# TensorE's instruction stream in loops, expert rows transposed by the transfer, and the split of the hidden layer shared between VectorE and ScalarE

## The chip, the cores and the metric

The kernel runs on one core of one Trainium2 chip. The metric is the device time of one execution in microseconds (us), lower is better. The engines of the core are TensorE (PE; its weight loads are PEld), VectorE (DVE), ScalarE (ACT), GpSimd (POOL) and SyncE (SP); each has its own instruction queue ("q" behind its name in a row), and they meet only through semaphores.

## The reference

Two layers on x of 16 batches x 512 nodes x 128 features. The first is a graph attention (4 heads) with an adjacency mask, added to x. The second is a mixture of 8 experts, each token going to its best two:

```python
x = x + gat(layernorm(x), adj, W, a)            # softmax over neighbours, 4 heads of 32
z = layernorm(x)
gate_scores = einsum('bsd,ed->bse', z, Wg) + bg
topk_scores, topk_idx = top_k(gate_scores, 2)
combine = softmax(topk_scores) spread over the 8 experts
for e in range(8):
    h = relu(z @ W1[e].T + b1[e])               # 128 -> 512
    y = h @ W2[e].T + b2[e]                     # 512 -> 128
    out = out + combine[..., e] * y
return x + out
```

## The kernel before

One program with a hand-written stream for each engine. The first stage works in **slots**: slot s has the attention of batch s in its front part and the second normalisation, the routing and the placing of batches s-1 to s-4 behind it. `slots(eng, body, ahead, end)` unrolls a body for each slot, on TensorE 18 of them, two of which only drain. Inside TensorE's `body` the products of several batches are interleaved by hand: transposes, `products`, `gate`, `broadcast`, the row sums in pieces (`sums`) and `ranks`. Many have a wait whose value depends on the batch (`hold`, `ge`, `pe.wait_ge`); with the slots unrolled these values are constants. GpSimd writes the normalised rows of every token twice to DRAM (`xs`, L469), grouped by expert; a row is 128 high halves and 128 low halves in fp16 (together 128 fp32 words) and two fp32 words, the token's number and its first expert.

The second stage runs over `BLOCKS` = 71 **expert steps**. A block is 256 rows of one expert. Which rows and which expert a block has is in `tab`, which VectorE fills in two parts (`tab_ready` 1 for blocks 0 to 40, 2 from `FULL` = 41 on). The engines work at different blocks in one step n:

- SyncE (`load_rows`, L397 to 402) reads block n's row number from `tab` and loads its 256 rows (130 KB) into `xb`, one of four buffers. It first waits for the transposes (`bt_ready`) and the index (`bidx_ready`) of block n-4.
- TensorE (`layers`) transposes block n+3 (X, four transposes, L1529) into PSUM, then makes the up product of block n+2 (U, L1543): for each of four chunks of 128 hidden units three matmuls of 256 columns (high x high, high x low, low x high). Then it reads the expert number of block n+3 from `tab` (`expert`, L1514; numbers read before are handed on in `held`), and last makes the down product of block n (Y, L1560): 24 matmuls.
- ScalarE (`hidden`) copies the transposed rows to SBUF (`xt`, L662) and applies bias and ReLU to the up product, four activations into `h32` (L673).
- VectorE (`work`) computes the target rows (`bidx`, L1232), casts all of `h32` to fp16 (`hp[..., 0]`, L1222), subtracts to get the low half (L1224), and takes the down product out of PSUM into `ysb` (L1239), one of four buffers.
- GpSimd (`send`) scatters `ysb` to DRAM in two indirect transfers (L519); VectorE's output of block n+4 waits for them.

The order on TensorE in a step is thus transposes, up product, table read, down product, and the down product of a block comes two steps after its up product. The steps from -3 to 2 are laced with the last batches' routing; GpSimd scatters the last batches' rows between its first sends. After step 70 the results are loaded back, weighted, added to x and stored.

All steps and slots are unrolled in before. The one loop is SyncE's, which loads the adjacency of batches 2 to 15 in seven rounds of two (L388, the loads at L379). The class `Batch` holds a number that can be an integer or, in a loop, an expression of the round.

## Time and profile before

| | |
|---|---|
| median of 3 runs | 625.65 us (623.48 to 626.25) |
| the profiled execution | 624.53 us |
| its span, first to last instruction | 622.6 us |
| mean granted clock of TensorE | 0.928 of full speed |
| TensorE matmul busy | 477.3 us (77% of the span) |
| TensorE weight loads busy | 435.4 us (70%) |
| VectorE busy | 515.9 us (83%) |
| ScalarE busy | 447.7 us (72%) |
| GpSimd busy | 402.5 us (65%) |
| instructions | 22344 |

Busy time leaves out register, branch and semaphore instructions, and matmul ends are modelled. Behind a group or an instruction the profile writes the idle time of its engine before it and, with an arrow, who ended it; "issue" means that the engine waited for nothing that the profile shows. Shares over the whole span mix the slots, the expert steps and the final stage; the rows below are from parts of it.

### The profile page before, as it was taken

What the parts mean: (1) busy time and instruction counts of PE and PEld (TensorE: products, weight loads), DVE (VectorE), ACT (ScalarE), POOL (GpSimd) and SP (SyncE); (2) the same over time, 40 slices, a digit from 0 to 9 for tenths busy, and PEclk for the clock granted to TensorE, in tenths of its full rate; (3) what the DMA queues carried; (4) which work ended last, traced back from release to release, by engine and by line L of the source; (5) the groups of instructions that cost most, each with busy time, mean ns of one, the idle gap of its engine ahead of it and who ended that gap; (6) DMA issues with size and microseconds to landing.
All of it is one profiled execution on the core that took longest, in us unless ns stands there. A gap on an engine that the chain in (4) does not pass through costs nothing.

```text
span 622.6 us, 22344 instructions
## 1 busy us (share of the span) xinstructions
PE 477.3 (77%) x7450; PEld 435.4 (70%) x7509; DVE 515.9 (83%) x1619; ACT 447.7 (72%) x908; POOL 402.5 (65%) x342
## 2 busy tenths in 40 slices
PE   0687887977888787988867866799999999997000
PEld 0576787867888777988766755688888888887000
DVE  4689998999999999999988984678788888886297
ACT  1585778878888888998717745678888888884264
POOL 2241235887777777787776787878778887887300
PEclk9997999889989999999896998999999999999555
DMA  8922221222222233231113252233333323331499
GB/s 312 399 107 68 70 70 34 73 98 96 95 75 64 93 106 99 96 100 37 37 45 83 76 147 78 79 90 89 88 88 93 88 79 91 86 86 37 136 367 307
DMA packets 60781, 67.92 MB, mean 109 GB/s; under 512 B 7267, under 2 KB 46318, under 8 KB 60417
## 3 DMA queue, kind: packets, MB, share of 16 engines
q1 hardware_dynamic: 41936, 44.31, 22.9%
q0 software_dynamic: 8816, 17.46, 8.4%
q10 hardware_dynamic: 9920, 4.73, 2.6%
q8 instruction: 66, 1.08, 0.8%
q14 instruction: 43, 0.34, 0.2%
HBM read 44.16 MB, written 23.22 MB: 108 GB/s over the span
## 4 chain that ended last, share of the span: by engine, by line
issue 31%; DVE 29%; POOL 15%; PE 9%; DMA 8%; ACT 6%; POOLq 1%; SPq 1%; DVEq 0%; ACTq 0%
POOL expert_out L519 13%; PE bank L1369 4%; DVE edge L816 4%; DVE bs L719 3%; ACT xn L575 3%; DVE G L824 3%; DMA G<-in_L_ffn_W 2%; PE bank L1360 2%; DVE mv L722 2%; DMA adji<-expert_out 2%; POOL expert_rows L469 2%; DVE T L833 2%; DVE rowt L863 1%; DVE sc L759 1%; DMA G<-expert_out 1%
## 5 line engine op out<-in xcount | busy, mean ns | idle before, releaser
L519 POOL DMA_INDIRECT expert_out<-late,bidx x142 | 170.1, 1198 | 43.3 <-issue 42.7
L469 POOL DMA_INDIRECT expert_rows<-rowt,idx x128 | 156.6, 1223 | 40.6 <-issue 35.7
L570 ACT ACTIVATE G<-bank,s2c 128x512 uint8<-128x512 f32 x256 | 153.7, 703 | 0.0
L673 ACT ACTIVATE late<-bank,b1s,sc 128x256 f32<-128x256 f32 x284 | 137.3, 563 | 13.0 <-PE bank L1543 12.5
L1369 PE MATMUL bank<-V,G 128*128 128x66 bf16 x3072 | 131.1, 198 | 4.0 <-ACT G L570 0.5
L1369 PEld LDWEIGHTS bank<-V,G 128*128 128x128 fp8e4 x3072 | 121.0, 100 | 8.8 <-issue 1.6
L1560 PE MATMUL bank<-W2h,G 128*128 x1704 | 107.6, 220 | 20.2 <-DVE late L1239 18.7
L1560 PEld LDWEIGHTS bank<-W2h,G 128*128 128x128 f16 x1704 | 97.4, 98 | 36.2 <-issue 35.8
L1543 PE MATMUL bank<-late,W1h 128*128 128x256 f16 x852 | 107.1, 277 | 0.0
L1224 DVE TENSOR_TENSOR G<-late,G 128x1024 f16<-128x1024 f32 x71 | 87.0, 1226 | 2.4
L1543 PEld LDWEIGHTS bank<-late,W1h 128*128 x852 | 81.6, 99 | 9.1
L1360 PE MATMUL bank<-V,edge 128*128 128x132 bf16 x768 | 62.5, 234 | 26.5 <-DVE T L833 26.3
L1222 DVE CAST G<-late 128x1024 f16<-128x1024 f32 x71 | 49.7, 700 | 38.5 <-ACT late L673 38.5
L662 ACT ACTIVATE late<-bank 128x512 f16<-128x512 f16 x71 | 42.4, 597 | 42.4 <-PE bank L1529 38.6
L1360 PEld LDWEIGHTS bank<-V,edge 128*128 128x128 fp8e4 x768 | 53.0, 102 | 28.3 <-issue 28.1
L575 ACT ACTIVATE xn<-xr,nb,rs 128x128 f32<-128x128 f32 x128 | 51.7, 480 | 27.4 <-DVE nb L810 19.6
L459 POOL TENSOR_TENSOR V<-V 128x1056 f32<-128x1056 f32 x16 | 31.2, 1948 | 60.9 <-DVE V L941 50.6
L1239 DVE SCALAR_TENSOR_TENSOR late<-bank,sc,b2b 128x256 f32<-128x256 f32 x71 | 34.0, 479 | 9.7 <-DMA expert_out<-late,bidx 8.3
L824 DVE TENSOR_TENSOR G<-G,edge 128x2048 uint16<-128x2048 uint16 x32 | 38.8, 1212 | 0.6 <-ACT G L570 0.6
L1391 PE MATMUL bank<-Wr,xnT 128*128 128x128 f32 x128 | 31.4, 337 | 0.8 <-ACT xnT L594 0.7
L719 DVE BATCH_NORM_STATS2 bs<-xr 128x6 f32<-128x128 f32 x128 | 28.9, 277 | 3.7 <-DMA xr<-in_x 3.7
L1529 PE MATMUL bank<-identh,V 128*128 128x128 f16 x284 | 28.3, 223 | 0.0
(166 smaller groups left out, 688.9 us busy)
## 6 DMA issues: line engine op xcount, KB each, us to landing
adji<-in_adj SPq DMA_DIRECT2D x16, 1024.0 KB
V<-expert_rows SPq DMA_DIRECT2D x71, 130.0 KB
adji<-expert_out SPq DMA_DIRECT2D x8, 512.0 KB, 5.8
G<-expert_out SPq DMA_DIRECT2D x8, 512.0 KB, 8.4
expert_out<-late,bidx POOLq DMA_INDIRECT x142
G<-in_L_ffn_W SPq DMA_DIRECT2D x1, 2048.0 KB, 13.4
late<-in_L_ffn_W SPq DMA_DIRECT2D x1, 2048.0 KB, 10.1
expert_rows<-rowt,idx POOLq DMA_INDIRECT x128
```

The lines of the kernel that those rows point to most:

```text
L469: pool.indirect_dma_start(xs, bass.IndirectOffsetOnAxis(ap=idx[:, Z.q, k, j:j + 1], axis=0), rowt[:, Z.q, j, :], None).then_inc(scattered[ ...
L519: pool.indirect_dma_start(ybuf, bass.IndirectOffsetOnAxis(ap=bidx[:, B.o, t:t + 1], axis=0), ysb[:, B.q, t, :], None, bounds_check=2 * TOK ...
L570: act.activation(Gs[:, M.p, h // 2, mt, :, h % 2], zb[h][:, :], ACT.Sign, bias=s2c[:, M.p, mt, h:h + 1]).then_inc(S["z_used"], 1)
L575: act.activation(dst[:, j, :], src[:, j, :], ACT.Identity, bias=nb[:, bass.ds(first + j, 1)], scale=rs[:, bass.ds(first + j, 1)]).then_inc ...
L673: act.activation(h32[:, U.p, c, :], Up[U.p][c // 2][:, (c % 2) * BLK:(c % 2 + 1) * BLK], ACT.Relu, bias=b1s[:, bass.ds(ex * NC + c, 1)], s ...
L824: dve.tensor_tensor(w, w, edge[:, M.p].rearrange("p t n -> p (t n)"), ALU.bitwise_and) \
L1222: c.did(dve.tensor_copy(hp[:, U.q, 0], h32[:, U.p]))
L1224: c.did(dve.tensor_tensor(hp[:, U.q, 1], h32[:, U.p], hp[:, U.q, 0], ALU.subtract))
L1360: mm(o[:, :, HD + 1:VW], edge8[:, R.p, mt, nt * P:(nt + 1) * P], v[:, :, HD + 1:VW], start=(mt == 0 and q == 0), stop=False, skip_group_ch ...
L1369: last = mm(o[:, h, :], G8[:, R.p, h // 2, mt, nt * P:(nt + 1) * P, h % 2], v[:, h, :], start=False, stop=(part == H and mt == NT - 1 and ...
L1543: last = mm(o, w, xt[:, U.p, xq, :], start=(n == 0), stop=(n == 2))
L1560: last = mm(Yp(Y)[:, t, :], hp[:, Y.q, hq, c, t * P:(t + 1) * P], w[wq], start=(c == 0 and n == 0 and t == 0), stop=(c == NC - 1 and n == ...
```

## The change

Six edits, which belong together.

- TensorE's slots 6 to 15 become a loop of five rounds of two slots; slots 0 to 5 and the last two stay unrolled.
- TensorE's expert steps 17 to 64 become a loop of six rounds of eight steps (`UNROLL`); the others stay unrolled. In the first step of a round, and in step 65, the expert numbers of the blocks n, n+1 and n+2 are read again (`at.first`). TensorE waits for the second part of `tab` once before the loop.
- The rows of a block are loaded by a transposing transfer straight into `xt`, now four buffers, and the two words of each row by a second, plain transfer into `xb`. TensorE's four transposes and ScalarE's copy fall away; the up product waits for the transfers itself. SyncE waits for the up product of block n-4 in place of its transposes.
- VectorE makes the high halves of three of the four chunks, by a reduction over an axis of length 1 in place of the cast, as soon as three activations are done.
- ScalarE makes the high half of the fourth chunk with a fifth activation straight from PSUM; VectorE's subtraction waits for it.
- Counts of `hid_ready` and `ld_rows` change to match.

```diff
...
 SHARED = 16
+LOOP_STEP = SHARED + 1
+UNROLL = 8
+LOOPS = (BLOCKS - 3 - LOOP_STEP) // UNROLL
+LOOP_SLOT = 6
 SCALES = 17
...
 LN_STEPS, S_STEPS, MX_STEPS, ARG_STEPS, X_STEPS, ATT_STEPS, ROUTE_STEPS, PLACE_STEPS = 8, 5, 2, 6, 2, 4, 13, 9
...
         h32 = late[:, 0:2 * NC * BLK].rearrange("p (a c n) -> p a c n", a=2, c=NC)
...
             .rearrange("p (a q c n) -> p a q c n", a=4, q=2, c=NC)
-        xb = V[:, 0].rearrange("p q t h v -> p (q t h v)")[:, 0:4 * BT * ROW].rearrange("p (b t w) -> p b t w", b=4, t=BT)
+        xt = V[:, 0].rearrange("p q t h v -> p (q t h v)")[:, 0:4 * BLK].bitcast(FP16) \
+            .rearrange("p (a q n) -> p a q n", a=4, q=2)
+        xb = V[:, 0].rearrange("p q t h v -> p (q t h v)")[:, 4 * BLK:4 * BLK + 8 * BT].rearrange("p (b t w) -> p b t w", b=4, t=BT)
         ysb = late[:, 2 * NC * BLK:2 * NC * BLK + 4 * BT * D].rearrange("p (b t d) -> p b t d", b=4, t=BT)
-        xt = late[:, 2 * NC * BLK + 4 * BT * D:2 * NC * BLK + 4 * BT * D + 2 * BLK].bitcast(FP16) \
-            .rearrange("p (a q n) -> p a q n", a=2, q=2)
         bidx = sb("bidx", [P, 8, BT], I32)
...
             adji[:, :, :, :].rearrange("p a t n -> p (a t n)").bitcast(F32)
...
-            return XTb[1 if B.n < SHARED else B.p]
+            return XTb[1 if isinstance(B.n, int) and B.n < SHARED else B.p]
...
-            return Yb[1 if B.n < SHARED else B.p]
+            return Yb[1 if isinstance(B.n, int) and B.n < SHARED else B.p]
...
         names = """ld_const ld_small ld_w1 ld_w2 ld_x0 ld_x1 ld_x2 ld_adj0 ld_adj1
...
                 body(Batch(n))
...
-        def step(n):
-            return lambda k: Batch(n + k) if 0 <= n + k < BLOCKS else None
+        def step(n, first=False):
+            at = lambda k: Batch(n + k) if 0 <= n + k < BLOCKS else None
+            at.first = first
+            return at
+        def looped_step(u, i):
+            at = lambda k: Batch(LOOP_STEP + u + k, i, UNROLL)
+            at.first = u == 0
+            return at
+        def is_block(B, n):
+            return isinstance(B.n, int) and B.n == n
+        def early(B):
+            return isinstance(B.n, int) and B.n < SHARED
...
             eng.wait_ge(S["ends_ready"], 1)
...
                 sp.wait_ge(scattered[k], 16 * 2 * NT * EARLY // 4)
...
             def load_rows(B):
-                ge(sp, S["bt_ready"], B.n - 3)
+                ge(sp, S["up_ready"], (B.n - 3) * NC)
                 ge(sp, S["bidx_ready"], B.n - 3)
                 r = sp.value_load(tab[0:1, 0, bass.ds(B.n, 1)], min_val=0, max_val=E * CAP)
-                sp.dma_start(xb[:, B.q], xs[bass.ds(r, BLK), :].rearrange("(t p) w -> p t w", p=P)) \
+                sp.dma_start(xt[:, B.q], xs[bass.ds(r, BLK), 0:D].bitcast(FP16), transpose=True) \
+                  .then_inc(ld_rows[B.q], 16)
+                sp.dma_start(xb[:, B.q], xs[bass.ds(r, BLK), D:ROW].rearrange("(t p) w -> p t w", p=P)) \
                   .then_inc(ld_rows[B.q], 16)
...
                 if n == FULL:
...
                 X, U = at(3), at(2)
-                if X:
-                    act.wait_ge(S["bt_ready"], X.n + 1)
-                    ge(act, S["up_ready"], (X.n - 1) * NC)
-                    if X.n == 0:
-                        act.wait_ge(S["w_dve"], 2 * PIECES)
-                    act.activation(xt[:, X.p], XTp(X), ACT.Copy).then_inc(S["xt_ready"], 1)
                 if U:
...
                     if U.n == 0:
...
                         act.activation(h32[:, U.p, c, :], Up[U.p][c // 2][:, (c % 2) * BLK:(c % 2 + 1) * BLK],
...
                            .then_inc(S["hid_ready"], 1)
+                    ge(act, S["down_ready"], U.n - 3)
+                    act.activation(hp[:, U.q, 0, NC - 1], Up[U.p][1][:, BLK:2 * BLK], ACT.Relu,
+                                   bias=b1s[:, bass.ds(ex * NC + NC - 1, 1)], scale=sc[:, 10:11]) \
+                       .then_inc(S["hid_ready"], 1)
             b13, b14, b15 = Batch(NB - 3), Batch(NB - 2), Batch(NB - 1)
...
             copy_x2T(b14)
...
-                dve.wait_ge(S["hid_ready"], U.n * NC + NC)
+                dve.wait_ge(S["hid_ready"], U.n * (NC + 1) + NC - 1)
                 ge(dve, S["down_ready"], U.n - 3)
                 c = Chain(dve, S["split_steps"], 2, U.n)
-                c.did(dve.tensor_copy(hp[:, U.q, 0], h32[:, U.p]))
+                c.did(dve.tensor_reduce(hp[:, U.q, 0, 0:NC - 1], h32[:, U.p, 0:NC - 1].unsqueeze(3), AX.X, ALU.max))
+                dve.wait_ge(S["hid_ready"], U.n * (NC + 1) + NC + 1)
                 c.wait()
...
                 U, Y = at(2), at(0)
...
-                    dve.wait_ge(ld_rows[U.q], U.f * 16 + 16)
+                    dve.wait_ge(ld_rows[U.q], U.f * 32 + 32)
                     ge(dve, back[U.q], (U.f - 1) * 16 * BT)
-                    dve.scalar_tensor_tensor(bidx[:, U.o, :], xb[:, U.q, :, D + 1], tf[:, 5, bass.ds(U.n, 1)],
-                                             xb[:, U.q, :, D], ALU.not_equal, ALU.add).then_inc(S["bidx_ready"], 1)
+                    dve.scalar_tensor_tensor(bidx[:, U.o, :], xb[:, U.q, :, 1], tf[:, 5, bass.ds(U.n, 1)],
+                                             xb[:, U.q, :, 0], ALU.not_equal, ALU.add).then_inc(S["bidx_ready"], 1)
                     split(U)
...
                     ex = dve.value_load(tab[0:1, 1, bass.ds(Y.n, 1)], min_val=0, max_val=E - 1)
...
                     ge(pe, S["route_steps"], (m4.n - 1) * ROUTE_STEPS + 1)
...
                         pe.wait_ge(S["place_steps"], m5.n * PLACE_STEPS + 3)
-                    if m4.n == 0:
+                    if at.s == 4:
                         pe.wait_ge(S["scale_steps"], 3)
...
                 if at.s == 3:
...
                     sums(m1, 0, 3)
...
                     weight_rows()
-            slots(pe, body, 0, NB + 2)
+            def at_slot(n, i=None):
+                if i is None:
+                    at = lambda k: Batch(n + k) if 0 <= n + k < NB else None
+                    at.s = n
+                else:
+                    at = lambda k: Batch(n + k, i)
+                    at.s = None
+                return at
+            for n in range(LOOP_SLOT):
+                body(at_slot(n))
+            with pe.Fori(0, (NB - LOOP_SLOT) // 2) as i:
+                body(at_slot(LOOP_SLOT, i))
+                body(at_slot(LOOP_SLOT + 1, i))
+            for n in range(NB, NB + 2):
+                body(at_slot(n))
...
             def layers(at):
...
                 X, U, Y = at(3), at(2), at(0)
-                if X:
-                    pe.wait_ge(ld_rows[X.q], X.f * 16 + 16)
-                    ge(pe, S["xt_ready"], X.n if X.n < SHARED else X.n - 1)
-                    if X.n == 0:
-                        pe.wait_ge(S["v_steps"], NB * X_STEPS)
-                    if X.n == SHARED:
-                        pe.wait_ge(S["xn2T_ready"], NB)
-                    xv = xb[:, X.q, :, 0:D].bitcast(FP16).rearrange("p t (q d) -> p t q d", q=2)
-                    for q in range(2):
-                        for t in range(BT):
-                            last = pe.transpose(XTp(X)[:, q, t * P:(t + 1) * P], xv[:, t, q, :], identh[:, :])
-                    last.then_inc(S["bt_ready"], 1)
-                ey, ex = held[0], held[2]
+                ey, ex = held[0], expert(U) if at.first else held[2]
                 if U:
-                    if U.n == 0:
+                    if is_block(U, 0):
                         pe.wait_ge(S["w_dve"], 2 * PIECES)
...
                         pe.wait_ge(S["t_steps"], NB * NT)
-                    pe.wait_ge(S["xt_ready"], U.n + 1)
-                    ge(pe, S["hid_ready"], (U.n - 1) * NC)
+                    pe.wait_ge(ld_rows[U.q], U.f * 32 + 32)
+                    ge(pe, S["hid_ready"], (U.n - 1) * (NC + 1))
                     for c in range(NC):
...
                             w = W1h[:, wq, bass.ds(ex, 1), c * P:(c + 1) * P].rearrange("p e h -> p (e h)")
-                            last = mm(o, w, xt[:, U.p, xq, :], start=(n == 0), stop=(n == 2))
+                            last = mm(o, w, xt[:, U.q, xq, :], start=(n == 0), stop=(n == 2))
                         last.then_inc(S["up_ready"], 1)
-                if X and X.n == FULL:
-                    pe.wait_ge(S["tab_ready"], 2)
+                if at.first:
+                    ey = expert(Y)
+                    held[1:] = [expert(at(1)), ex]
                 held[:] = held[1:] + [expert(X) if X else None]
                 if Y:
-                    if Y.n == 0:
+                    if is_block(Y, 0):
                         pe.wait_ge(S["arg_steps"], NB * ARG_STEPS)
                         pe.wait_ge(S["rows_ready"], NB)
-                    if Y.n == SHARED:
+                    if is_block(Y, SHARED):
                         pe.wait_ge(S["place_steps"], NB * PLACE_STEPS)
                     pe.wait_ge(S["split_steps"], Y.n * 2 + 2)
-                    ge(pe, S["y_ready"], Y.n if Y.n < SHARED else Y.n - 1)
+                    ge(pe, S["y_ready"], Y.n if early(Y) else Y.n - 1)
                     for c in range(NC):
...
                         for n, (hq, wq) in enumerate(((0, 0), (1, 0), (0, 1))):
...
             layers(step(1))
...
             ranks_after(b15)
-            for n in range(3, BLOCKS):
+            for n in range(3, LOOP_STEP):
                 layers(step(n))
+            pe.wait_ge(S["tab_ready"], 2)
+            with pe.Fori(0, LOOPS) as i:
+                for u in range(UNROLL):
+                    layers(looped_step(u, i))
+            for n in range(LOOP_STEP + LOOPS * UNROLL, BLOCKS):
+                layers(step(n, n == LOOP_STEP + LOOPS * UNROLL))
...
 _INS = ["x", "adj", "L0_gnn_W", "L0_gnn_a", "L0_ffn_Wg", "L0_ffn_bg", "L0_ffn_W1", "L0_ffn_b1", "L0_ffn_W2", "L0_ffn_b2"]
```

## Rows read from the trace of the kernel before

**Rows 1.** Waits, 200 to 300 us: us in total, times, longest.

```profile
PE bank L1360 <- DVE T L833: 8.9, 6, 2.2
...
PE bank L1405 <- DVE mxp L899: 4.3, 5, 0.9
...
DVE g L959 <- PE bank L1398: 0.6, 1, 0.6
```

**Rows 2.** Windows: length, busy us (instructions) of PE, PEld, DVE, ACT, POOL; clock, DMA.

```profile
404.00:566.00 162.00, 160.14 (x2129) 141.92 (x2130) 129.99 (x213) 134.06 (x266) 129.40 (x108) 1.00 0.31 86
```

**Rows 3.** Timeline of TensorE's weight loads: start, us, what, idle before.

```profile
404.52 1.35 PEld L1560 LDWEIGHTS bank<-W2h,G 128*128 128x128 f16 x24 [1.34 <-issue]
...
486.39 1.35 PEld L1560 LDWEIGHTS bank<-W2h,G 128*128 128x128 f16 x24 [0.16 <-issue]
...
487.93 1.25 PEld L1543 LDWEIGHTS bank<-late,W1h 128*128 x12
489.51 0.18 PEld L1560 LDWEIGHTS bank<-W2h,G 128*128 128x128 f16 x3 [0.34 <-issue]
...
565.51 1.36 PEld L1560 LDWEIGHTS bank<-W2h,G 128*128 128x128 f16 x24 [0.30 <-issue]
...
568.08 2.77 PEld L1560 LDWEIGHTS bank<-W2h,G 128*128 128x128 f16 x48
```

**Rows 4.** TensorE's queue by line, 486.3 to 489.42 us: ns min/median/max, first and last start.

```profile
L1560 PEldq ALU_OP  x8: 32/32/32, 486.3 to 487.1; - x8
...
L1543 PEldq FUSED_REGOPS  x8: 46/46/46, 487.7 to 488.5; - x8
...
L1514 PEldq TENSOR_LOAD <-tab x1: 303/303/303, 488.7 to 488.7; - x1
```

**Rows 5.** Timeline of all engines, the end of the expert steps.

```profile
574.02 0.48 DVE L1239 SCALAR_TENSOR_TENSOR late<-bank,sc,b2b 128x256 f32<-128x256 f32 x1 [1.35 <-PE bank L1560]
...
581.92 0.98 POOL L519 DMA_INDIRECT expert_out<-late,bidx  x1 [0.30 <-issue]
```

**Rows 6.** Timeline, single instructions: reductions, transfers, cast and activations.

```profile
17.69 4.42 DVE L759 TENSOR_REDUCE sc<-G 128x1 f32<-128x4096 f32 x1 [1.27 <-DMA G<-in_L_ffn_W]
...
344.65 1.96 POOL L469 DMA_INDIRECT expert_rows<-rowt,idx  x1 [1.10 <-DVE rowt L1022]
...
364.09 0.99 POOL L519 DMA_INDIRECT expert_out<-late,bidx  x1 [0.31 <-issue]
...
364.57 0.41 DVE L1054 TENSOR_REDUCE tf<-cube 128x31 f32<-128x248 f32 x1
...
451.51 0.69 DVE L1222 CAST G<-late 128x1024 f16<-128x1024 f32 x1 [0.57 <-ACT late L673]
451.60 1.46 POOL L519 DMA_INDIRECT expert_out<-late,bidx  x1 [0.30 <-issue]
...
452.60 1.93 ACT L673 ACTIVATE late<-bank,b1s,sc 128x256 f32<-128x256 f32 x4 [0.16 <-PE bank L1543]
```

**Rows 7.** Waits, 342 to 404 us.

```profile
PE bank L1560 <- DVE late L1239: 16.3, 10, 3.5
DVE late L1239 <- DMA expert_out<-late,bidx: 8.3, 4, 3.6
```

**Rows 8.** SyncE's queue, the loop of adjacency loads (L388, L379).

```profile
L388 SPq FUSED_REGOPS  x7: 50/50/64, 24.4 to 236.2; - x7
...
L388 SPq COMPARE_BRANCH  x7: 44/45/50, 46.4 to 270.8; - x7
...
L379 SPq FUSED_REGOPS  x14: 46/46/57, 32.3 to 270.2; - x14
```

**Rows 9.** Waits of SyncE's queue over the whole span.

```profile
SPq L107 <- DVE bidx L1232: 142.2, 65, 6.4
```

**Rows 10.** DMA view: a queue (packets, MB, share); an issue (KB, us to landing).

```profile
q8 instruction: 66, 1.08, 0.8%
...
xr<-in_x SPq DMA_DIRECT2D x1, 256.0 KB, 2.9
```

## The prediction

> **What bounds the kernel now.** The program has stages with different limits, so I first cut its span into windows. The attention slots run to about 320 us, the expert steps from 342 to 575 us, and then come the last loads, sums and stores, which the change leaves alone. In the slots the waits tell the bound: VectorE waits once in 100 us, for 0.6 us, while TensorE waits 8.9 us for VectorE's sums and 4.3 us for its row maxima [rows 1]. At some 18 us a slot (seven rounds of two slots in SyncE's loop, 46 to 271 us [rows 8]) that is 2.4 us of slack a slot on TensorE.
>
> From 404 to 566 us TensorE is "busy" 160 of 162 us [rows 2], but its ends are modelled, so I read its weight loads instead. The loads of the down product begin at 404.52 and, 53 steps later, at 565.51 us: 3.04 us a step [rows 3]. In one step, the down product and the four transposes take 486.39 to 487.93, the up product 1.25 us, and then comes a gap of 0.34 us that no engine releases ("issue"); the step before had one of 0.16 [rows 3]. The last full step with neither a transpose nor a table read goes from 565.51 to 568.08 with no gap: 2.57 us [rows 3]. So neither the array nor another engine is the bound; TensorE's own sequencer is. The same step in its queue [rows 4]: eight register operations of the down product start from 486.3 to 487.1, a pitch of 0.12 us and 0.96 in all; waits and transposes fill the time from there to 487.7, where eight fused register operations of the up product follow at the same pitch, another 0.96; then the table read for a later step starts at 488.7, and its check and a wait last until just before the next down product's first load at 489.51 [rows 3]. Nothing stands still. From the two products I solve the prices. Down: 48 loads and matmuls and 8 x 0.032 us in 0.96, so an array instruction costs 0.0147 us. Up: 24 x 0.0147 and eight fused operations in 0.96, so one of these costs 0.076, its gap included. A table read costs 0.7 us.
>
> The other engines have room. VectorE is busy 130 of 162 us, 2.45 a step, and waits for ScalarE the rest; ScalarE 134 us [rows 2]. GpSimd's gaps are all "issue", never data, yet it stays two sends behind: after the last output (574.02 + 0.48) its last transfer starts at 581.92 [rows 5], so it ends at 582.9.
>
> **Transposes and copy go.** TensorE's sequencer loses what fills 487.26 to 487.7 [rows 4], less one wait that stays: about 0.30 us. ScalarE loses one copy a step and gains a fifth activation of 1.93 / 4 = 0.48 us [rows 6]: about even, and off the path. An unrolled step would cost 3.04 - 0.30 = 2.74 us.
>
> **The split.** The cast of 1024 elements (0.69 us [rows 6]) becomes a reduction of 768. Reductions take 4.42 us for 4096 elements and 0.41 for 248 [rows 6]: 1.04 ns an element and 0.15 fixed, so 0.95 us, 0.26 more. VectorE's step becomes 2.45 + 0.26 and some 0.1 for semaphores, 2.8 us: below TensorE's pace, free in the loop, but the floor of an unrolled step. What it buys is GpSimd's time. A send that begins under the cast (451.60, cast from 451.51) lasts 1.46 us; one with a reduction inside it (364.57, in the send of 364.09) lasts 0.99 [rows 6]. But the subtraction that follows the cast holds sends as well: the transfer of 344.65, begun just after a subtraction had started, takes 1.96 us [rows 6]. So GpSimd can stay stretched and two sends behind. At the end: a send right after the last output would finish at 574.5 + 0.3 + 2.3 = 577.1 instead of 582.9, so 0 to -5.8 us; I take -2, nearer to nothing since the subtraction stays. From 342 to 404 us TensorE waits 16.3 us for VectorE's output, 8.3 of it because VectorE waits for sends [rows 7]; against that gain stands 0.26 us more on VectorE in a dozen steps. +3 to -8 us; I take -3.
>
> **The expert loop.** 48 of the 71 steps (17 to 64) become six rounds of eight. Their wait values (rows landed, activations, split, outputs) and the table address now depend on the round: five quantities a step. The nearest row is SyncE's loop of adjacency loads: two waits and two addresses a round, for which seven rounds pay 14 + 7 fused operations, three for four quantities [rows 8]. That makes 3.75 x 0.076 = 0.28 us a step; bounds 0.1 (values shared within a round) and 0.38. At the head of each round three expert numbers that unrolled code carries over are read again: 3 x 0.7 = 2.1 us, 0.26 a step. The loop's own counter and branch are one operation each in eight steps, 0.01. The step becomes 3.04 - 0.30 + 0.28 + 0.26 + 0.01 = 3.29 us, over VectorE's floor of 2.8, and +0.25 x 48 = +12 us. Nothing covers it: the array already waits for this sequencer in each step. Queued behind are the up product, ScalarE's activations, the split, the outputs and the sends. Step 65 repeats the three reads (+2.1), and some six unrolled steps at full pace gain 0.25 each (-1.5). The wait for the table's second half moves from step 38 to step 17; VectorE sets that flag after its sixth step, so it costs nothing.
>
> **The slot loop.** Ten slots become five rounds of two. Some 40 waits a slot get register values: at 3/4 of 0.05 to 0.076 us, 1.5 to 2.3 us of sequencer, against 2.4 us of waiting [rows 1]. Most of it hides there, but VectorE has no idle time to absorb results that come late. Bounds 0 and +1 us a slot; I take +0.3, +3 us in all.
>
> **The transfers.** SyncE waits mostly for VectorE's index, 142 us over 65 loads [rows 9], so the queue has time, for a second transfer too. The rows are now used by the up product, one step after the transposes used them, so the load's lead grows by about 3 us, and the load waits for an up product three rows back, which is done when the index is. The trace has no transposing transfer; bounds: a plain load like today's, or one longer than a step. I take the first, zero. The Trainium skill ("Advanced Engine Details and Errata", X-Bar Transpose) says that transposing transfers on trn2 are as fast as ordinary ones; no row here shows it, and it would leave the sum as it is.
>
> **Sum.** +12 + 2.1 - 1.5 + 3 - 3 - 2 = +10.6, on the profiled run's 624.5 us (its span of 622.6 and 1.9 around it) 635; that run stands 1.1 below the median of 625.65, so 636.
>
> **Rivals.** (1) *Refetched code*: each jump back must bring the loop's first instructions again while TensorE stands still. Its code came in 66 blocks over the span, which took 0.8% of 16 engines' time, 1.2 us each; a 256 KB load lands in 2.9 us [rows 10]. So 1.2 to 3 us a jump, six in the steps, and five in the slots, where waiting hides half: 636 + 6 x 2.5 + 5 x 1.2 = 657. The Trainium skill ("Runtime: NRT & Kernel Launch", Instruction fetch mechanics) says that a taken branch to a target outside the fetched window stalls until its page is there; SyncE's loop is too short to show it, and here the bodies are some 850 and 1,300 instructions. (2) *Half price*: wait values are shared and the reads at the head overlap the array's backlog. Then the step is 3.02 us, and the gains of ramp and end stand against the slots: 624. (3) *The sequencer is no bound once the transposes are gone*: VectorE's floor of 2.8 us sets the step, 54 x -0.24 = -13, with -5 before 404 us and -3 at the end: 604. This is the case on the other side; it decides if a looped step's register work and reads stay under 0.06 us. Against it stands the gap in every step; for it, that the fifth activation and the shorter reduction relieve VectorE, which pays only where VectorE is the bound, and that GpSimd has no idle time of its own now. (4) *The transposing transfer takes longer than a step*, say 4 us: TensorE waits for rows in 66 steps, 690. It decides above 3 us.
>
> **Chances.** Forecast 0.42 (its own range 628 to 650), refetch 0.14, half price 0.15, VectorE's floor 0.22, slow transfer 0.07. Within 0.5%, about what a measurement of this kernel can tell from no change, is 622.5 to 628.8: most of the half-price case and an edge of the forecast, 0.16; slower 0.56; faster 0.28. The range reaches from just below the fast case to the refetch case, 602 to 660.
>
> **What would show it.** Right: the first loads of the down product stand 3.0 to 3.1 us apart inside a round with some 2 us extra at every eighth, "issue" still before them, more fused operations a step and four table reads at a round's head; no send stretched to 1.46 by a cast. Wrong: gaps released by a row load (rival 4), several us of nothing at every eighth step (rival 1), or steps of 2.8 us with VectorE never idle (rival 3). In the slots the period tells whether the register work was hidden.

## The result, and the profile after

The changed kernel takes 640.75 us (median of four runs, 638.05 to 644.46); the kernel before took 625.0 beside it. The ratio is 1.026, 95% interval 1.020 to 1.032: slower by 16 us. The forecast was 636 in a range of 602 to 660. The profiled execution has a span of 639.9 us against 622.6, so 17.3 us have to be found in the trace.

The timeline of TensorE's weight loads in the changed kernel (start, us, what, idle before; L1585 is the down product, L1567 the up product) answers [rows 3]:

```profile
401.85 1.35 PEld L1585 LDWEIGHTS bank<-W2h,G 128*128 128x128 f16 x24 [0.84 <-issue]
...
442.51 1.56 PEld L1585 LDWEIGHTS bank<-W2h,G 128*128 128x128 f16 x24 [2.33 <-issue]
444.02 2.39 PEld L1567 LDWEIGHTS bank<-V,W1h 128*128 x12
...
547.30 1.35 PEld L1585 LDWEIGHTS bank<-W2h,G 128*128 128x128 f16 x24 [0.47 <-issue]
549.61 1.21 PEld L1567 LDWEIGHTS bank<-V,W1h 128*128 x12 [0.96 <-issue]
553.14 0.95 PEld L1585 LDWEIGHTS bank<-W2h,G 128*128 128x128 f16 x17 [2.32 <-issue]
...
574.64 1.35 PEld L1585 LDWEIGHTS bank<-W2h,G 128*128 128x128 f16 x24 [0.47 <-issue]
576.58 1.21 PEld L1567 LDWEIGHTS bank<-V,W1h 128*128 x12 [0.59 <-issue]
579.93 1.34 PEld L1585 LDWEIGHTS bank<-W2h,G 128*128 128x128 f16 x24 [2.14 <-issue]
...
588.44 2.78 PEld L1585 LDWEIGHTS bank<-W2h,G 128*128 128x128 f16 x48
```

The first and the last row here are the same products as 404.52 and 568.08 before, 54 steps apart in both. That cuts the span into three parts:

| | until the first | 54 steps | behind the last | span |
|---|---|---|---|---|
| before | 404.5 | 163.6 | 54.5 | 622.6 |
| after | 401.9 | 186.6 | 51.5 | 639.9 |
| difference | -2.7 | +23.0 | -3.0 | +17.3 |

All of the loss lies in the middle part, which holds the looped steps and step 65. Inside a round a step takes 3.05 us, as before (3.04); in the first round it is 3.1 to 3.4. The head of each round is what is new: 547.30 to 553.14 is 5.84 us, with 0.96 us of nothing ahead of the up product and 2.32 ahead of the down product, both "issue": nobody released them. Rounds take 27.4 to 28.3 us, 3.47 a step, where eight steps took 24.3. Step 65 reads the table again too, but the branch ahead of it does not jump: 574.64 to 579.93, 5.29 us. The step behind a head takes some 0.2 more than the others (3.22 for the one of 553.14), and at 442.51 it took 3.97: its twelve up loads need 2.39 us and not 1.21. The granted clock shows why:

```profile
436.64:442.51 5.87, 2.98 (x36) 2.44 (x37) 4.00 (x8) 3.97 (x9) 4.46 (x5) 1.00 0.35 78
442.51:446.48 3.97, 3.96 (x36) 3.29 (x37) 1.83 (x3) 0.73 (x2) 1.29 (x2) 0.63 0.27 56
```

(Windows of the changed kernel: length, busy us of PE, PEld, VectorE, ScalarE, GpSimd; granted clock, DMA.) The array was busy for 3.0 of the head's 5.9 us, and in the next step the granted clock stood at 0.63: most of that step ran at the lower level, 1.2 GHz. It happened behind two of the seven heads, this one and that of 470.50. Why the clock fell there is not shown: the head of 547.30 has the same 2.98 us of busy array in 5.84 us, and behind it the clock stayed at 1.00.

TensorE's queue in one step inside a round, 562.35 to 565.42 us (ns min/median/max, first and last start), answers [rows 4]:

```profile
L1585 PEldq ALU_OP  x8: 32/32/32, 562.4 to 563.2; - x8
...
L1567 PEldq FUSED_REGOPS  x8: 46/46/51, 563.4 to 564.3; - x8
...
L1550 PEldq FUSED_REGOPS  x2: 46/98/151, 564.4 to 564.9; - x2
L1550 PEldq TENSOR_LOAD <-tab x1: 311/311/311, 564.5 to 564.5; - x1
```

And at the head of a round, 547.30 to 553.14 us, four reads, the last three in a row. L1621 is the loop, the branch here over all six rounds (only the last does not jump, 76 ns); the down product behind a head has fused register operations, where the other steps of the round have the shorter ALU_OP:

```profile
L1621 PEldq COMPARE_BRANCH  x6: 76/208/209, 437.6 to 575.6; - x6
...
L1550 PEldq TENSOR_LOAD <-tab x4: 299/302/308, 548.7 to 552.2; - x4
...
L1585 PEldq FUSED_REGOPS  x8: 46/46/46, 553.0 to 554.0; - x8
```

In this queue the loop's counter, branch and address take 0.49 us until the first read starts, that read 0.64, and the two that follow each other behind the up product 0.75 each: 2.6 of the 2.8 us that a head takes more than a plain step.

The waits from 404 to 580 us name no transfer. They give 12.3 us ahead of the down product to VectorE's reduction and 5.2 ahead of the up product to ScalarE's fifth activation, at the heads. Both names mislead. The down product of 553.14 needs the split of its own block, which VectorE ended at 547.64; until 552.8 TensorE's queue was at its reads. The transposing transfer hides. Its SyncE instruction takes 1.21 us where the plain one took 0.37, and packets under 512 bytes rise from 7,267 to 64,066, yet SyncE still waits for VectorE's index:

```profile
L421 SPq DMA_TRANSPOSE V<-expert_rows x71: 1207/1213/2397, 325.8 to 576.0; - x71
...
SPq L107 <- DVE bidx L1253: 47.6, 57, 2.7
```

The instruction queue, which carried 66 blocks before [rows 10], now carries 30:

```profile
q8 instruction: 30, 0.49, 0.3%
```

So the code of these loops was fetched once, and no jump back fetched it again.

### The profile page after: what moved, and what is told of

Its sections match the earlier page's. It is cut to its first block, busy times and chain, and to the rows that moved or that the text cites. A ratio compares the mean times of both kernels' runs of the same rounds, so it can differ in the third digit from the quotient of the medians.

```text
span 639.9 us, 22307 instructions
## 1 busy us (share of the span) xinstructions
PE 473.7 (74%) x7225; PEld 422.9 (66%) x7226; DVE 533.5 (83%) x1619; ACT 438.2 (68%) x908; POOL 391.0 (61%) x342
## 2 busy tenths in 40 slices
DMA packets 99368, 67.34 MB, mean 105 GB/s; under 512 B 64066, under 2 KB 84941, under 8 KB 99040
## 4 chain that ended last, share of the span: by engine, by line
DVE 39%; PE 22%; issue 17%; ACT 9%; DMA 7%; ACTq 3%; DVEq 1%; POOL 1%; SPq 1%; POOLq 0%
PE bank L1585 8%; PE bank L1567 6%; DVE G L1242 5%; DVE G L1245 4%; ACT late L689 4%; DVE edge L836 3%; PE bank L1390 3%; DVE bs L739 3%; DVE G L844 3%; PE bank L1381 2%; ACT xn L597 2%; DMA G<-in_L_ffn_W 2%; DVE mv L742 2%; DVE T L853 2%; DMA adji<-expert_out 2%
## 5 line engine op out<-in xcount | busy, mean ns | idle before, releaser
L541 POOL DMA_INDIRECT expert_out<-late,bidx x142 | 160.1, 1128 | 73.7 <-issue 42.5
L1585 PE MATMUL bank<-W2h,G 128*128 x1704 | 109.8, 222 | 42.8 <-DVE late L1260 18.2
L1585 PEld LDWEIGHTS bank<-W2h,G 128*128 128x128 f16 x1704 | 99.6, 99 | 59.6 <-issue 59.3
L1567 PE MATMUL bank<-V,W1h 128*128 128x256 f16 x852 | 111.6, 284 | 5.2 <-ACT G L693 5.2
L1242 DVE TENSOR_REDUCE G<-late 128x768 f16<-128x768 f32 x71 | 67.6, 952 | 39.1 <-ACT late L689 38.9
L1567 PEld LDWEIGHTS bank<-V,W1h 128*128 x852 | 83.8, 102 | 17.5 <-issue 6.4
L693 ACT ACTIVATE G<-bank,b1s,sc 128x256 f16<-128x256 f32 x71 | 40.9, 575 | 0.0
L1367 PE MATMUL bank<-rows,selb 128*128 128x512 bf16 x64 | 26.3, 411 | 2.6 <-ACT rows L626 1.4
```

The source lines that it names most:

```text
L541: pool.indirect_dma_start(ybuf, bass.IndirectOffsetOnAxis(ap=bidx[:, B.o, t:t + 1], axis=0), ysb[:, B.q, t, :], None, bounds_check=2 * TOK ...
L1242: c.did(dve.tensor_reduce(hp[:, U.q, 0, 0:NC - 1], h32[:, U.p, 0:NC - 1].unsqueeze(3), AX.X, ALU.max))
L1567: last = mm(o, w, xt[:, U.q, xq, :], start=(n == 0), stop=(n == 2))
L1585: last = mm(Yp(Y)[:, t, :], hp[:, Y.q, hq, c, t * P:(t + 1) * P], w[wq], start=(c == 0 and n == 0 and t == 0), stop=(c == NC - 1 and n == ...
```

## The experiments

The theory at the start: TensorE's sequencer sets the step, so each register operation, table read and jump that a loop adds to its stream lengthens it. The rivals: another engine or the transfers set the step, or code is fetched anew at each jump.

### Loop and rounds

**The expert steps written out** (a1), slots still looped:

```
-            with pe.Fori(0, LOOPS) as i:
-                for u in range(UNROLL):
-                    layers(looped_step(u, i))
-            for n in range(LOOP_STEP + LOOPS * UNROLL, BLOCKS):
-                layers(step(n, n == LOOP_STEP + LOOPS * UNROLL))
+            for n in range(LOOP_STEP, BLOCKS):
+                layers(step(n))
```

> The changed kernel with its expert steps unrolled again (slots still in a loop, no numbers read twice, wait values constant). Theory: TensorE's sequencer sets the step and the loop's extra work is what made the change slow; the loop step of the changed kernel averages 3.42 us (a round of eight in 27.4), unrolled it falls to VectorE's floor of about 2.8 to 2.85 us, 47 x -0.57 = -27, so about 614 us. Rival A: in the changed kernel something else holds the step near 3.0 us (its unrolled steps 65 to 67 stand 2.97 apart), then 47 x -0.44 = -21, about 620. Rival B: the loop is not the cause, about 640.

Measured 613.5 us, ratio to the kernel before 0.984 (0.981 to 0.987). So the loop of the expert steps, with the second reading of step 65, costs 27 us, and the rest of the change gains 10.

**Rounds of 16 and of 4**: `UNROLL = 16` (a3), `UNROLL = 4` (a4).

> The changed kernel with 16 steps in a round, three rounds in place of six, the same 48 steps. Theory: a round's head costs 27.4 - 8 x 3.04 = 3.1 us over its steps, whatever the length of the round: three heads fewer, -9, about 631 us. Rival (refetched code): a jump back costs nothing at 850 instructions but several us where the body of about 1,700 does not stay loaded; then more instruction blocks are fetched (over 40 in place of 30) and the time stays at 640 or rises.

> The changed kernel with four steps in a round, twelve rounds in place of six. Theory: six more heads of 3.1 us, +18.6, about 659 us. If the head's cost is mostly hidden behind VectorE's and ScalarE's queues, less than half of that, under 650.

Measured 631.35 (1.012, 1.009 to 1.015) and 659.51 (1.059, 1.055 to 1.063). With step 65's, the three kernels have 4, 7 and 13 heads: (640.75 - 631.35) / 3 = 3.13 us a head, and (659.51 - 640.75) / 6 = 3.13 again. A straight line, at all three body lengths. That the two agree to the digit is luck, since the changed kernel's interval is 7 us wide; a3 and a4, which were compared with the same executions of the kernel before, give 28.16 / 9 = 3.13 by themselves. Taken back to no head it gives 618.8; the written-out kernel has 613.5, and the 5.3 between them, over 48 steps, are 0.11 us a step for the wait values. The instruction queue carries 33 and 29 blocks. That settles refetching (rival 1): no body of 4, 8 or 16 steps was brought again. The Trainium skill ("Runtime: NRT & Kernel Launch", Instruction fetch mechanics) has a taken branch stall when its target lies outside the fetched window, and gives TensorE room for 2,048 instructions; the longest body here has 1,539 in the trace, so by that room the condition was not met. The same section of the Trainium skill also speaks of a window of two pages of 256 instructions; by that it was met in bodies of 777 and 1,539, and no run shows the stall.

**A second table read in each step of the kernel before** (b1):

```
...
-                held[:] = held[1:] + [expert(X) if X else None]
+                held[:] = held[1:] + [(expert(X), expert(X)) if X else (None, None)]
...
```

> The kernel before, with every expert number read twice in a step, once for the up and once for the down product; nothing else changes. Theory: TensorE's sequencer has no slack in a step, so each step at full pace grows by a table read, 0.7 us: 53 x 0.7 = +37, and a part more before 404 us, about 662 us. Rival: the array, VectorE or GpSimd sets the 3.04 us and the sequencer only looks full; then a second read hides at least in part, under 640.

Measured 662.39 (1.064, 1.060 to 1.067); the steps lengthen from 3.04 to 3.80, by 0.76 us. Not all of it is the read. In the queue (b1, 489.4 to 491.9 us) the second read starts 0.65 us after the first, and the eight register operations of the down product have become fused ones (51 or 46 ns, 32 before), 0.13 us more in the mean of 22 steps:

```profile
L1514 PEldq TENSOR_LOAD <-tab x2: 308/309/310, 489.5 to 490.1; - x2
...
L1560 PEldq FUSED_REGOPS  x8: 46/46/51, 490.9 to 491.8; - x8
```

So a read with its check costs 0.65 us of TensorE's time, and 0.75 with an address operation of its own. Nothing hides it, nor the 0.13.

**The loop alone in the kernel before** (b2), as a1's diff read backwards, with transposes, copy, cast and slots untouched:

> The kernel before with its expert steps 17 to 64 as six rounds of eight and nothing else changed: transposes, copy, cast and slots stay. Theory (costs of loop and transposes add up on TensorE's sequencer): a step inside a round 3.04 + 0.30 = 3.34 us, a head 2.1 + 0.37 us more: 14.4 + 14.8 + 2.1 for step 65 on 625 is 656, within 3. Rival (taking the transposes out gained nothing; they stood beside other work): what the change costs here is all there is, 17.6 + 2.1: 645.

Measured 656.55 (1.056, 1.051 to 1.062), as the sum says: what a loop adds comes on top of the transposes.

### The other parts

**The slots written out as well** (a2):

```
...
-            with pe.Fori(0, (NB - LOOP_SLOT) // 2) as i:
-                body(at_slot(LOOP_SLOT, i))
-                body(at_slot(LOOP_SLOT + 1, i))
+            for n in range(LOOP_SLOT, NB):
+                body(at_slot(n))
...
```

> The changed kernel with both of TensorE's loops written out, steps and slots; everything else as changed. Theory (the slot loop's register work is hidden behind TensorE's waits for VectorE): the same as with the steps alone written out, 613.5 within 1.5 us. The recorded prediction (the slot loop costs 3 us): 610.5.

Measured 614.0 (0.985, 0.980 to 0.990) against a1's 613.5: the slot loop costs nothing that these times can show. Their intervals would hide the forecast 3 us; the traces are sharper, and the last part has what they say.

**The split undone** (a7): a2 without the fifth activation, and with the old cast. What is left of the change is the transfer that transposes.

```
...
-                c.did(dve.tensor_reduce(hp[:, U.q, 0, 0:NC - 1], h32[:, U.p, 0:NC - 1].unsqueeze(3), AX.X, ALU.max))
-                dve.wait_ge(S["hid_ready"], U.n * (NC + 1) + NC + 1)
+                c.did(dve.tensor_copy(hp[:, U.q, 0], h32[:, U.p]))
...
```

> As a2_all_unrolled, and the split undone: no fifth activation of ScalarE, VectorE casts all 1024 elements again. Theory (with the expert steps written out VectorE is what sets the step, at about 2.9 us, and the reduction costs it 0.26): VectorE's work falls to 2.64, the sequencer's 2.74 becomes the bound, 0.16 us in each of some 60 steps, less 3 us at the end for GpSimd's stretched sends: 604 to 608. Rival (TensorE's sequencer sets the step at 2.9): no gain in the steps, and the stretched sends are lost: 613 to 617.

**A cast of 768 elements in place of the reduction** (a5), the rest as a2.

> As a2_all_unrolled, but the 768 elements of the split's high halves are cast and not reduced; ScalarE still writes the rest. Theory (VectorE sets the step): its work falls by 0.43 us, the sequencer sets the step at 2.74: 603 to 607. If GpSimd's sends, which a cast holds, set the pace instead: 613 or more. Rival (the sequencer sets 2.9 already): 613 to 616.

Measured 616.91 (0.991, 0.987 to 0.994) and 614.71 (0.986, 0.981 to 0.991). My theory fell here. It had VectorE as the bound of the written-out step; VectorE's work fell by 9% and by 14%, and the step stayed at 2.90 us in all three; the rival's 613 to 617 is what came. From 465 to 549 us:

```profile
465.00:549.00 84.00, 81.46 (x1047) 70.89 (x1045) 78.13 (x116) 69.21 (x146) 61.86 (x58) 1.00 0.48 89
```

is a2 (VectorE 78.1 us), and

```profile
465.00:549.00 84.00, 81.49 (x1046) 70.87 (x1044) 67.02 (x117) 69.22 (x145) 66.31 (x59) 1.00 0.46 90
```

is a5 (67.0), with the same number of products. GpSimd shows what the reduction does: 58 sends take 61.9 us in a2 and 59 take 66.3 in a5, but GpSimd is not what the step waits for. SyncE these three kernels do not exclude, since all have its two transfers a block; c2 below does, which changes TensorE's reads alone and whose commonest step is 2.65 us. The sequencer is what is left. Its segments, from the starts of the first register operations of each product and of the table read, means over three or four steps:

| us | down product (and transposes) | up product | read, to the next step | step |
|---|---|---|---|---|
| before | 1.21 | 1.08 | 0.78 | 3.06 |
| a2, written out | 1.08 | 1.05 | 0.78 | 2.90 |
| after, inside a round | 1.08 | 1.10 | 0.88 | 3.05 |

### Fewer reads

If the sequencer is the bound, the loop need not cost anything: the reads can be made fewer. One table read can fill four registers, and the table is written as a minimum with E - 1, so its range check can go.

```
...
-                return pe.value_load(tab[0:1, 1, bass.ds(B.n, 1)], min_val=0, max_val=E - 1)
+                return list(nc.values_load_multi_w_load_instructions(
+                    tab[0:1, 1, bass.ds(B.n, n)], [pe.engine], min_val=0, max_val=E - 1,
+                    skip_runtime_bounds_check_because="written as min(., E - 1)")[1])
...
+                if at.first:
+                    held[:] = experts(Y, 3)
+                if X and (at.first or not ahead):
+                    ahead[:] = experts(X, at.read)
+                held[:] = held[1:] + [ahead.pop(0) if X else None]
...
```

**In the changed kernel, loops in place** (c1).

> The changed kernel, both loops in place; TensorE reads the expert numbers of four blocks with one table read without a range check, and the three of a round's head with another, so three reads a round where there were eleven. Theory (the loop costs time only because TensorE's sequencer is the bound, and eleven reads of 0.8 us a round are the largest part of it): the sequencer needs 2.2 us of products and 0.2 of reads a step, VectorE's 2.85 us sets the step, 48 x (3.42 - 2.87) = 26 us less: 614, between 608 and 618. Rival (the reads hide beside the array, and jumps and wait values are the cost): above 630.

Measured 609.01 us, 0.973 (0.970 to 0.975): 32 us faster than the changed kernel, and faster than the kernel before. A round takes 22.3 us, its head 3.7 to 4.0 and a step in it 2.65. In the steps the loads now follow one another without a gap (c1; L1592 down, L1575 up):

```profile
508.22 1.43 PEld L1592 LDWEIGHTS bank<-W2h,G 128*128 128x128 f16 x24
509.62 1.24 PEld L1575 LDWEIGHTS bank<-V,W1h 128*128 x12
510.87 1.21 PEld L1592 LDWEIGHTS bank<-W2h,G 128*128 128x128 f16 x20
```

The read of four (c1's queue, 499 to 512 us) takes hardly longer than that of one, 0.33 us against 0.31:

```profile
L1552 PEldq TENSOR_LOAD <-tab x2: 329/332/336, 499.7 to 509.9; - x2
```

Inside a round the array itself is the bound at last. I had VectorE's four operations down as 2.85 us; one begins before the other ends, so that it was busy 79.1 of the 84 us from 465 to 549 and kept up, with little room.

The edit does two things at once, fewer reads and no check, and no run separates them. In the queues a checked read takes 0.65 us and the unchecked read of four 0.39. An estimate from these: dropping the check alone, with one read a step, would bring the written-out step of 2.90 us to 2.64, as far as the reads of four did.

**The same with the expert steps written out** (c2), **and with the cast of a5** (c3).

> The same reads of four, expert steps written out, slots looped. Theory (VectorE's 2.85 us comes right behind the sequencer's 2.90): 613.5 less 60 x 0.05, 610 within 2. Rival (nothing stands behind the sequencer before the array's 2.6 us): 613.5 less 60 x 0.3, 596.

> As c2_unrolled_four, with VectorE casting the 768 elements where it reduced them. VectorE then has 2.45 us a step, but GpSimd's two sends, held by the casts, have 2.85. Theory (GpSimd sets the step next): 610 to 615, no better than with the reduction, and later at the end. Rival (VectorE alone mattered): 600 or less.

Measured 606.5 (0.972, 0.965 to 0.978) and 611.12 (0.975, 0.972 to 0.979). By the medians the loop now costs 2.5 us; c2's own runs spread by 8, so c1 and c2 can't be told apart. Nor is the difference a clean price of the loop: c2 has no heads, and yet its steps 17 to 64 take 2.79 us in the mean, as in c1. Most take 2.65, but ten take 2.8 to 4.6, the longest because the up product waits for its rows (c2; L423 is the transposing transfer, L425 the plain one, L1575 the up product):

```profile
466.44 1.22 SPq L423 DMA_TRANSPOSE V<-expert_rows  x1
...
467.85 0.43 SPq L425 DMA_DIRECT2D V<-expert_rows  x1
...
469.09 1.22 SPq L423 DMA_TRANSPOSE V<-expert_rows  x1
469.13 1.48 PE L1575 MATMUL bank<-V,W1h 128*128 128x256 f16 x12 [1.77 <-DMA V<-expert_rows]
```

SyncE's queue has become as full as the array: two issues, a table read and its check take it 2.65 us a block, here with nothing between them, and now and then a transposing issue takes longer (2.09 us at 457.23, up to 2.39 after 404 us, in place of 1.21). In c3 from 465 to 549 us TensorE waits

```profile
PE bank L1575 <- DMA V<-expert_rows: 5.3, 9, 0.9
```

for rows, 2.8 us in c2. Whether the casts, through GpSimd, have a part in that, as I had expected, is not shown. All three intervals overlap, so that the cast is the worse one here is not shown either.

**Four experts a read in the kernel before** (b3), nothing else changed.

> The kernel before, nothing looped, transposes and casts in place, with TensorE reading the expert numbers of four blocks at once. It asks what the reads alone are worth without the rest of the change. Theory A (TensorE's sequencer alone set the 3.04 us step): the step falls to the array's 2.75 or so, 54 x 0.29 = 16 us less: 609. Theory B (GpSimd, whose sends the casts and subtractions hold, stands right behind: its 57 sends with their gaps fill 87 us of the 84 between 465 and 549): the step stays at 2.9 to 3.04: 615 to 625.

Measured 615.94 (0.986, 0.980 to 0.991), a step of 2.87 us. The number is B's, the reason is neither's (b3; L1566 down, L1533 transposes, L1547 up):

```profile
508.38 1.44 PEld L1566 LDWEIGHTS bank<-W2h,G 128*128 128x128 f16 x24
509.77 0.27 PEld L1533 LDWEIGHTS bank<-identh,V 128*128 128x128 f16 x4
510.00 1.24 PEld L1547 LDWEIGHTS bank<-late,W1h 128*128 x12
511.25 0.82 PEld L1566 LDWEIGHTS bank<-W2h,G 128*128 128x128 f16 x13
```

No gap either: the array's own work, with the transposes in it, is 2.87 us and not my 2.75. Without them it is 2.65 (c1). GpSimd's 59 sends (66.9 us, the one at the window's edge counted whole) and the gaps between them (18.0) fill the 84 us here too, so it keeps pace exactly; that it would be the next bound is not excluded.

## Why the prediction came out as it did

**Direction, place and mechanism held.** The sequencer bounds the step (b1, c1), and the loss is the loop's (a1), most of it at the heads of rounds. Refetching (rival 1) is excluded by the 30 blocks and by the straight line through a3, the changed kernel and a4; VectorE's floor (rival 3) by a5 and a7; the slow transfer (rival 4) by the waits, for the changed kernel. Half price (rival 2) was right of the wait values and wrong of the heads, where no read hides. The step of 3.0 to 3.1 us inside a round came as forecast by luck, out of two terms each half as large as I had them. Luck has a part in the sum as well: the looped steps and step 65 were to cost 12 + 2.1 - 1.5 = 12.6 us and the middle part of the table cost 23.0, while the 3 us of the slot loop never came. The sizes:

| term | predicted, us | measured, us | from |
|---|---|---|---|
| transposes out, a step | -0.30 | -0.14 to -0.15 | a2 and a7 against before |
| wait values, a step | +0.28 | +0.11 to +0.15 | segments; a3, a4, a1 |
| a head, beyond a plain step | 2.1 | 3.1 to 3.4 | a3, a4; rounds |
| of it, three reads | 2.1 | 2.1 to 2.2 | queue |
| of it, the jump | 0.01 | 0.5 | queue |
| step in the loop, mean | 3.29 | 3.47 | rounds |
| slot loop | +3 | 0.3 | ten slots in all kernels |
| until 404 us | -3 | -2.7, slots included | timeline |
| end | -2 | -3.0 | timeline |
| six unrolled steps | -1.5 | about 0 | timeline |

**Transposes and copy go** was wrong in its size. I took 0.30 us from the queue of a single step, 486.3 to 489.42 [rows 4]. Its first segment lasts 1.33 us; in the next three steps it lasts 1.18 to 1.19, and 1.21 in the mean from 465 to 549 us. The gaps of 0.16 and 0.34 in two steps side by side [rows 3] should have warned me that steps differ, and that a mean over several was needed.

**The expert loop** was wrong in two sizes. The wait values cost half of what SyncE's loop made me expect. The head costs half as much again: I put down three reads of 0.7 us and 0.01 for the jump. The reads were right: 0.64 + 0.75 + 0.75 us in the queue. The jump was the term put at nothing, and it is 0.49 us: SyncE's branch takes 44 ns [rows 8], TensorE's 208 where it jumps, with a counter and an address operation around it. Besides, the step behind a head is 0.2 us longer, since its down product has fused register operations, and the clock was at its lower level after two heads of seven. Per step: -0.15 + 0.15 + 0.43 instead of -0.30 + 0.28 + 0.27.

**The slot loop** was wrong the other way. Its register work hid. From the third to the thirteenth load of `sel` and `trib` (L1438, L1417 before), ten slots apart, TensorE takes 175.1 to 176.2 us in the seven kernels here that loop the slots and 175.0 to 175.9 in the seven that don't, 0.3 us apart in the mean; and the waits from 200 to 300 us are near those of [rows 1], 9.8 us for T and 3.6 for mxp. My bounds had held zero, and the rows said that TensorE had 2.4 us of slack a slot; I should have taken the bound that the row gave.

**The split.** The reduction does spare the sends (1,118 ns the mean expert send from 465 to 549 us, 1,219 before), though one that begins beside the subtraction still takes up to 1.74 us. But the end does not hang on it much: the last send begins 13.8 us after the start of the last 48 weight loads (568.08) before and 11.2 after, and 11.2 to 11.3 in every kernel whose steps average above 3.2 us, with the reduction (a3, a4) or the cast (b1, b2). It is the slower pace that lets GpSimd catch up. At the fast pace it is 13.7 and 12.4 with the reduction (a1, a2), 12.6 and 14.8 with a cast (a7, a5). So the term's size was right and its reason mostly wrong. The ramp to 404 us comes out at 402.8 to 405.0 us where all is cast (before, a7, b1, b2, b3) and 400.3 to 402.8 in eight of the nine others, 404.2 in c3: two or three us for the split, transfers included. Taken whole it is worth 3 us (616.9 to 614.0), and the intervals overlap.

**The transfers** were forecast at zero, and in the changed kernel they were zero. The Trainium skill ("Advanced Engine Details and Errata", X-Bar Transpose) has transposing transfers as fast as ordinary ones on trn2. The trace shows no wait for one in the changed kernel, which is not the same; what it does show dearer is the issue on SyncE, 1.21 us against 0.37. It was free at this pace only: SyncE's wait for VectorE's index, 142.2 us before [rows 9], is 47.6 in the changed kernel and 10.9 in c2, where rows came late.

**Six unrolled steps.** Steps 11 to 16 run at 3.0 to 3.7 us, 3.35 in the mean, not at 2.8: their outputs share one buffer, and TensorE waits some 0.5 us a step for VectorE's output ahead of them (15.6 us from 342 to 404, where [rows 7] has 16.3). Relief for the sequencer is worth nothing there.

## What to carry to other kernels

Where the queue of an engine never stands still while its unit has gaps marked "issue", count its instruction stream in us before anything else: a loop pays there for each value that unrolled code has as a constant or carries in a register, and most at its head. The remedy is not the unrolling but the reads: one unchecked table read for four blocks made the looped kernel faster than the written-out one with a checked read a step (609.0 and 613.5 us). Then look at every queue again, since the next bound may be one that had room before: here SyncE's issues. And size a term by the mean of several periods, since one step can be off by twice the term that one wants.

## What was not expected of the hardware

- A checked table read costs TensorE's sequencer 0.65 us, 0.75 with its own address operation, of which the load itself is 0.3. A load that fills four registers takes 0.33, so it is the read and not the number that costs; the Trainium skill ("Runtime: NRT & Kernel Launch", Instruction fetch mechanics) has some 200 ns a register even in bulk, of loads from HBM, which is not what these loads from SBUF show. Three unchecked reads a round in place of eleven checked ones took 5.1 to 6.0 us off it (27.4 to 28.3 against 22.3).
- A jump back costs TensorE 0.49 us with its counter and address (the branch 208 ns, 76 where it does not jump), and a head as a whole 3.13, the same with bodies of 4, 8 and 16 steps.
- Behind a pause of 2.3 us at a head the granted clock can be down for a step (0.63 from 442.51 to 446.48 us), or not (1.00 from 498.40 to 501.65). In the changed kernel, a3, a4 and b2 it was down, 0.59 to 0.66, behind 13 of the 27 heads of rounds and behind none of the four of step 65; what decides it is not shown.
- An issue of the transposing transfer takes SyncE 1.21 us, and in c2 up to 2.39. With the plain one and the table read that made SyncE's 2.65 us a block level with the array's step in c2.
- GpSimd's sends with their gaps filled the whole time in the kernel before, in b3 and in c1, at 3.04, 2.87 and 2.79 us a step: an engine that is never idle need not be the bound.
